# Pre-norm decay attention and mixture of experts on one core: folds on another engine, and another order of the early loads

## What is computed

```
x = x + attn(layernorm(x));  x = x + moe(layernorm(x))

def attn(x):                       # 16 heads of 32
    q, k, v = split(x @ w_qkv, 3)
    q, k = elu(q) + 1, elu(k) + 1
    decay = sigmoid(decay_param)                       # one per head
    run_kv = scan(s = decay * s + k * v over tokens);  run_k = scan(s = decay * s + k)
    den = clip(sum(q * run_k over the head), 1e-6)
    return (q * run_kv / den) @ w_out

def moe(x):                        # 8 experts, the best 2 by softmax, hidden width 352
    scores = softmax(x @ gate_w);  top_w, top_idx = top_k(scores, 2)
    routed = sum over the two of top_w * (silu(x @ w_gate[e]) * (x @ w_up[e])) @ w_down[e]
    shared = (silu(x @ sw_gate) * (x @ sw_up)) @ sw_down      # hidden width 704
    return routed + shared
```

## Time and profile before

| | |
|---|---|
| median of 3 runs | 683.62 us (677.13 to 686.48) |
| the profiled execution | 681.28 us |
| its span in the profile | 679.5 us |
| TensorE busy | 646.2 us (95%) |
| VectorE busy | 416.2 us (61%) |
| ScalarE busy | 267.8 us (39%) |
| GpSimd busy | 222.7 us (33%) |

### The profile page before, as it was taken

How to read it: one execution, slowest core, us unless ns; L and a number is a source line. 1 busy time by engine, 2 the same in 40 slices (tenths; PEclk the granted TensorE clock), 3 DMA queues, 4 the chain that set the end, 5 groups by cost and what they waited for, 6 DMA issues and landing times.

```text
span 679.5 us, 11781 instructions
## 1 busy us (share of the span) xinstructions
PE 646.2 (95%) x3787; PEld 426.7 (63%) x3788; DVE 416.2 (61%) x754; ACT 267.8 (39%) x407; POOL 222.7 (33%) x266
## 2 busy tenths in 40 slices
PE   7989999999999999999998999999999999999991
PEld 7766777767677656666655656666666666666550
DVE  7786987997998755767778776533333333333330
ACT  5363462464453445465665765311111111111110
POOL 6320131231103227222332241244444444434421
PEclk9998999999999999999999999999999999999997
DMA  6840012513425697586684424388777877889852
GB/s 233 309 133 16 15 48 66 167 47 94 125 63 175 185 248 191 160 187 170 162 188 137 72 42 87 65 148 137 133 127 134 137 131 137 133 134 126 136 76 40
DMA packets 110388, 86.89 MB, mean 128 GB/s; under 512 B 79280, under 2 KB 85424, under 8 KB 110352
## 3 DMA queue, kind: packets, MB, share of 16 engines
q1 hardware_dynamic: 88848, 43.94, 27.9%
q0 software_dynamic: 12864, 29.50, 25.5%
q10 hardware_dynamic: 8640, 12.98, 5.8%
HBM read 44.45 MB, written 23.33 MB: 100 GB/s over the span
## 4 chain that ended last, share of the span: by engine, by line
PE 55%; DMA 10%; DVE 7%; issue 3%; ACT 1%; POOL 1%; SPq 1%; POOLq 0%; DVEq 0%; ACTq 0%
PE ps_y L535 15%; PE ps_u L535 14%; PE ps_g L535 14%; PE ring L393 8%; DMA out_dram<-y_job,job_tok 5%; PE turn_h L555 3%; DMA x_in<-x_job 2%; DMA x_job<-xn_scratch,job_tok 2%; DVE routed L1484 1%; DMA xn_scratch<-xn_hl 1%; DMA out_dram<-x 1%; DVE hid L1427 1%; DVE col_max L1463 1%; DVE den L1359 0%; PE ps_norm L410 0%
## 5 line engine op out<-in xcount | busy, mean ns | idle before, releaser
L1145 ACT CAST hidT<-turn_h 128x384 f16<-128x384 f32 x71 | 33.9, 478 | 173.1 <-PE turn_h L555 168.2
L989 POOL DMA_INDIRECT out_dram<-y_job,job_tok x39 | 61.8, 1585 | 98.9 <-DVE y_job L1769 60.0
L393 PE MATMUL ring<-xnT_h,wq_h 128*128 128x512 f32 x192 | 79.4, 413 | 4.2 <-DVE xnT_l L1298 2.0
L535 PE MATMUL ps_y<-routed,hidT 128*128 x351 | 82.1, 379 | 1.3 <-DVE hidT L1420 1.3
L535 PE MATMUL ps_g<-routed,x_in 128*128 x468 | 82.6, 313 | 0.5 <-DMA x_in<-x_job 0.5
L393 PE MATMUL ring<-xnT_h,wq_l 128*128 128x512 f32 x192 | 77.3, 403 | 0.0
L393 PE MATMUL ring<-xnT_l,wq_h 128*128 128x512 f32 x192 | 77.1, 402 | 0.0
L535 PE MATMUL ps_u<-routed,x_in 128*128 x468 | 76.2, 312 | 0.0
L1427 DVE SCALAR_TENSOR_TENSOR hid<-ps_u,job_hid,silu 128x352 f32<-128x352 f32 x39 | 22.8, 584 | 85.5 <-PE ps_u L535 83.3
L535 PE MATMUL ps_y<-shared,hidT 128*128 128x512 f16 x288 | 67.4, 379 | 3.7 <-DVE hidT L1420 3.7
L896 POOL TENSOR_SCALAR var_eps<-mean_var 128x1 f32<-128x1 f32 x32 | 12.3, 384 | 171.9 <-DVE mean_var L1406 93.4
(11 more groups left out here) (246 smaller groups left out, 1095.5 us busy)
## 6 DMA issues: line engine op xcount, KB each, us to landing
x_res<-in_L_attn_x_dram SPq DMA_DIRECT2D x18, 256.0 KB, 3.6
routed<-in_L_ffn_w_gate_dram ACTq DMA_DIRECT2D x6, 704.0 KB, 4.7
routed<-in_L_ffn_w_up_dram ACTq DMA_DIRECT2D x6, 704.0 KB, 6.5
out_dram<-x SPq DMA_DIRECT2D x16, 256.0 KB, 3.5
xn_scratch<-xn_hl SPq DMA_DIRECT2D x16, 256.0 KB, 2.6
out_dram<-y_job POOLq DMA_DIRECT2D x16, 256.0 KB
x_in<-in_L_attn_x_dram SPq DMA_DIRECT2D x14, 256.0 KB, 2.7
routed<-in_L_ffn_w_down_dram ACTq DMA_DIRECT2D x6, 512.0 KB, 7.2
```

The lines of the kernel that those rows point to most:

```text
L393: ins = pe.matmul(ps, a, b, start=(i == 0), stop=(i == len(steps) - 1))
L535: ins = pe.matmul(ps, a[i][:, k, :], w(j, k), start=(start and q == 0), stop=(stop and q == len(steps) - 1))
L989: pool.indirect_dma_start(out[:, :], bass.IndirectOffsetOnAxis(job_tok[:, r:r + 1], 0), y_job[:, b, :], None, compute_op=ALU.add).then_inc ...
L1145: act.copy(hidT[:, 0], turn_h[:, 0:FC, :]).then_inc(s["hidTh_s"], 1)
```

## The change

1. The 16 folds of routed gate and up matrices leave GpSimd; DVE does them at the end of the unit, behind the splits and ahead of the routing work.
2. Part 11 of the projection matrix gets a place of its own (`last_raw`, later used by the last shared down piece), so its load waits for nothing. Parts 12 to 15 wait for low parts by new counts, and the shared down matrix also waits for part 11's low part.
3. x tiles 4 to 7 are loaded ahead of the shared matrices, tiles 6 and 7 into `x_res`; the residual's first two tiles are loaded later, behind x tiles 8 and 9.
4. The four loads of the decay parameters go from GpSimd to ScalarE, as the first thing that it issues.
5. DVE makes the low parts of weight parts 2 and 3 behind those of all four x tiles.
6. The first projection (K of chunk 0) needs the four high parts to start, does its eight products with high weights first, and waits for one low part ahead of each of the last four. The waits of V and Q are as before.
7. In each block DVE makes the low part of the next block's second x tile ahead of `lo_gate` and `max_step`, not behind.

The diff, cut to its core:

```diff
+            if m == QKV_PARTS - 1:
+                return last_raw[:, 0:D]
+            return w_raw[:, (turn_of(m) % 3) * D:(turn_of(m) % 3 + 1) * D]
...
-            return (x_res if t in (2, 3) else x_in)[:, t % 2, :]
+            return (x_res if t in (2, 3, 6, 7) else x_in)[:, t % 2, :]
...
-                if n == 0 and c == 0:
-                    pe.wait_ge(s["w_lo"], KC * {1: 1, 2: 2, 0: 3}[z] - EARLY_W)
-                    pe.wait_ge(s["w_lo_e"], EARLY_W)
+                first = n == 0 and c == 0 and z == 1
+                if first:
+                    pe.wait_ge(s["w_hi"], KC)
+                elif n == 0 and c == 0:
+                    pe.wait_ge(s["w_lo"], KC * {2: 2, 0: 3}[z] - EARLY_W)
...
+                for k, ((wh, wl), (xh, xl)) in enumerate(pairs):
+                    pe.matmul(ps[:, :], wh, xh, start=(k == 0), stop=False)
+                    pe.matmul(ps[:, :], wh, xl, start=False, stop=False)
+                for k, ((wh, wl), (xh, xl)) in enumerate(pairs):
+                    if k < EARLY_W:
+                        pe.wait_ge(s["w_lo_e"], k + 1)
+                    else:
+                        pe.wait_ge(s["w_lo"], k + 1 - EARLY_W)
+                    ins = pe.matmul(ps[:, :], wl, xh, start=False, stop=(k == KC - 1))
...
             def load_x(t):
                 if t >= TPB:
-                    sp.wait_ge(s["xn1"], t - 1)
+
+                    sp.wait_ge(s["xn1"], t - 3 if t < 2 * TPB + 2 else t - 1)
...
             def load_part(m):
-                if m >= FREE_PARTS + 3:
-                    sp.wait_ge(s["w_lo"], m - 2 - EARLY_W)
+                if m >= QKV_PARTS:
+
+                    sp.wait_ge(s["w_lo"], m - 3 - EARLY_W if turn_of(m) < 6 else m - 2 - EARLY_W)
...
-            load_res(0)
-            load_res(1)
-            load_x(TPB)
-            load_x(TPB + 1)
+            for t in range(TPB, 2 * TPB):
+                load_x(t)
...
             sp.wait_ge(s["over_0"], 1)
+            sp.wait_ge(s["w_lo"], QKV_PARTS - EARLY_W)
...
+                if n == 0:
+                    load_x(2 * TPB)
+                    load_x(2 * TPB + 1)
+                    load_res(0)
+                    load_res(1)
...
-            for g in range(P // DH):
-                pool.dma_start(dec[g * DH:(g + 1) * DH, :], bass.AP(decay.tensor, g, [[0, DH], [P // DH, KC]]),
-                               allow_slow_non_contiguous=True).then_inc(s["dec_in"], 16)
...
-                for u in (2 * t, 2 * t + 1):
-                    if norm_unit(u) is not None and pieces[norm_unit(u)][1] < 2:
-                        fold(norm_unit(u))
...
+            for g in range(P // DH):
+                act.dma_start(dec[g * DH:(g + 1) * DH, :], bass.AP(decay.tensor, g, [[0, DH], [P // DH, KC]]),
+                              allow_slow_non_contiguous=True).then_inc(s["dec_in"], 16)
...
             lo_x(1)
-            lo_w(EARLY_W)
             lo_x(2)
-            lo_w(EARLY_W + 1)
             lo_x(3)
-            for m in range(TPB, QKV_PARTS):
+            for m in range(EARLY_W, QKV_PARTS):
                 lo_w(m)
...
                 query(n, 2)
+                next_x(lo_x, 1)
                 if n == 0:
                     lo_gate()
                 max_step(n * KC + 2)
-                next_x(lo_x, 1)
...
-                if norm_unit(u) is not None and pieces[norm_unit(u)][1] == 2:
+                if norm_unit(u) is not None:
                     fold(norm_unit(u))
```

42 lines of the change are left out of this document (22 added, 20 removed).

## The result

The changed kernel took 673.13 us (median of 5 runs, 671.50 to 676.39), the kernel before 684.84 (median of 5 runs, 677.13 to 686.48). The ratio is 0.988, with a 95% interval of 0.984 to 0.992. Beside the first experiments the same two kernels ran again, and gave 672.99 us (6 runs), 681.29 us (14 runs) and a ratio of 0.989 [0.986, 0.993]. The medians of the first pair differ by 11.7 us, more than its ratio says, and those of the second by 8.3. The profiled execution took 676.39 us (span 674.3) against 681.28 (span 679.5) before.

The account below looks back on a forecast made before the run. TensorE was taken as the bound, so time is won only where it stands or runs slowly. 3.4 - 0.3 + 4.2 + 2.7 = 10.0 us off the median of 683.62 gave 673.6 us, range 667 to 681.

Parts of the forecast that it names:

- Start: Up to the first query projection: it starts at 20.1 instead of 23.46 us, 3.4 us won; bounds 0.6 and 3.7.
- x tiles that land clearly later than before: At the kernel's beginning: one of the listed signs that would show the forecast wrong; no size given.
- The decay loads: Moved to ScalarE's queue, they run while the x tiles land: 0.3 us lost, bounds 0 and 2.8.
- The upper bound of 2.8: Loads of decay parameters: 2.8 us per engine if each of 512 four-byte elements cost an average packet of the other queue.
- rival (d): Beginning of the kernel: the decay loads hold up the x tiles, 2.8 in place of 0.3 us, total 676.1; chance 5%.
- Block 0: First block: wait for tile 5's low part shrinks by 2.5 us, clock returns 1.7: 4.2 us won, bounds 1.3 and 4.7.
- Folds: Mixture: folds on DVE save 1.8 us of hidT waits and 0.9 of a fold wait: 2.7 us; upper bound 4.7.
- (a): Mixture: DVE stands at each fold for the square, 16 x 1.59 = 25.4 us lost, total 701.7; chance 3%.
- (b): Value projection: waits 1.3 us or more and runs at 1.2 GHz, 2.8 us lost, total 676.4; chance 14%.
- (c): First block stays bound by DVE and the clock still falls: 1.3 instead of 4.2 us, total 676.5; chance 12%.
- (e): Whole kernel: all waits go, 3.7 + 4.7 + 4.7 = 13.1 us won, total 670.5; chance 10%.
- a threshold between 1.69 and 1.97 us: TensorE's clock: a pause of 1.69 us did not bring it down, only 1.97 and 3.04 did.

Follow-up runs that it names:

- the first experiments: First group of follow-up runs, on one chip with the kernel before: the changed kernel repeated unchanged (ratio 0.989), and e1, e2 and e4, which move the decay loads.
- e5: Changed kernel with the sixteen folds of routed gate and up back on GpSimd; ratio to the kernel before 0.993.
- e2: Changed kernel with the four decay loads issued by SyncE, behind the last part of the projection weights; 672.62 us, ratio to the kernel before 0.987.
- e11: e2 run once more, unchanged, on another chip; median 675.68 us, ratio to the kernel before 0.990.
- e4: Kernel before with only the four decay loads moved, from GpSimd to the head of ScalarE's queue; 684.43 us against 681.29, ratio 1.006.
- e1: Changed kernel with the four decay loads back on GpSimd, behind its low parts of the weights; 672.89 us, ratio to the kernel before 0.988.
- e12: Changed kernel with decay loads behind SyncE's weight parts and each scatter ahead of the gather for the job four later; 692.59 us, ratio to the kernel before 1.017.
- e6: Changed kernel with the low part of the next block's second x tile back behind the gate's low part and column maximum; ratio to the kernel before 0.991.
- e8: Changed kernel with weight part 11 back in the ring of three buffers, its load waiting for part 8's low part; ratio to the kernel before 0.989.
- e9: Changed kernel with x tiles 6 and 7 loaded behind the shared matrices, in the buffers the change gave them; ratio to the kernel before 0.994.
- e10: Changed kernel with decay loads behind SyncE's weight parts and GpSimd making three low parts of the projection weights instead of two; ratio to the kernel before 0.990.

## Why the prediction was right, and where it was not

The time was forecast at 673.6 us and is 673.13. That they agree so closely is partly luck: the ratio makes it 1.2% and 1.1%, about 8.3 and 7.3 us of the time before, where the forecast had 10.0. The marks say the same, with 7.5 and 6.8 us at mark B in the two traces. The forecast was set against a median of 683.62 us for the kernel before, which came out at 684.84 in this measurement and at 681.29 in the next.

**Start: 3.4 us forecast.** The query projection, which follows the value projection's 2.8 us without a wait, starts near 22.6 instead of 23.46: 0.85 us won, and 0.5 in the second trace. The working itself was sound, since without the decay loads it came out at 13.30 and 17.64 against the forecast 13.2 and 17.3. The prediction had named x tiles that land clearly later than before as a sign of being wrong, and they did. The parts that it was built from are each worth something by themselves: undoing the order costs 1.45 us, undoing the buffer 1.80.

**The decay loads: 0.3 us forecast. This is the step that failed.** I put them near the row that showed these very loads, 128 packets on GpSimd's queue. On ScalarE's queue they are 576 packets, and it is not the engine time they take (3.5% from 2 to 10 us) that costs, but what they do to the queue beside them: 1.22 MB in place of 2.38. By the kernel before, the move costs 2.5 us at mark A. With the change made, mark A has a mean of 71.3 over the three traces with this start (71.47, 71.81 and e5's 70.58), and of 69.8 over the three with the loads at SyncE and nothing else changed in the start (69.34, 70.74, 69.29): 1.5 us.

Part of that is the clock during the warm-up, which has to be taken out. In both traces of the changed kernel 14 warm-up matmuls took 1.70 us (1.2 GHz), against 0.94 in e5 and e2. But e11, with the loads away, has the 1.70 too, and is 1.4 us later at mark A than e2, which is the same kernel. Compared at equal clock, mark A is 1.3 us later at the full clock (70.58 against 69.34 and 69.29) and 0.7 to 1.1 at the lower one (71.47 and 71.81 against 70.74). The first projection is 1.5 us later at the full clock (e5's 14.77 against 13.30 and 13.22), of which 1.0 to 1.1 is the late x tile. A warm-up with matmuls at 1.2 GHz behind the first transposes' pause is found in five of the eight traces with the loads at ScalarE's head, where TensorE pauses 1.71 to 2.62 us ahead of its first transposes, and in one of the six others, with pauses of 0.68 to 0.81. So the longer pause may make it more frequent; that is not shown. The marks also miss something: an execution is 2.01 to 2.16 us longer than its span wherever the loads are at ScalarE's head, and 1.71 to 1.84 elsewhere, 0.3 us more that lie outside the span.

The upper bound of 2.8 and rival (d) held the truth, and (d) had got 5%. The Trainium skill (DMA: Bandwidth & Descriptors, Rules for kernel authors) was weighed against the row of GpSimd's queue in the prediction, and the measurement sides with the skill: 576 is 512 four-byte elements and four times 16. The row was of another queue, and that should have made it weigh less.

**Block 0: 4.2 us forecast, 3.9 found** (4.7 at mark A less 0.85, and 4.4 less 0.5). The wait is 0.75 us where 0.55 was forecast, and the clock stays at 1.00 as forecast. Its rows add up: the wait is 2.29 us shorter (3.04 to 0.75, where 2.5 was forecast), and from the transposes behind it to the next ones it takes 3.26 us in place of 4.82, so 1.56 come from the clock (1.7 forecast). What the prediction said of the parts is half right. The order is worth the 1.6 us that was read from DVE's rows. The early x tiles were counted at 1.32 us and are worth 3.7: 2.1 of wait, since DVE gets to the tile earlier than before and would stand for it all the longer, and 1.55 of clock.

**Folds: 2.7 us forecast, 3.5 to 3.9 found** by the single undo. Each step is in the trace: y_scale at 0.16 us, DVE's busy time down though it does more, the wait for a fold 1.69 to 0.34. Both terms were too small: the waits for hidT were forecast to lose 1.8 of 3.0 us and lost 2.6, the wait for a fold 0.9 and lost 1.35. That the whole change shortens the way from A to B by only 2.8 us (325.15 to 322.34), near the 2.7 forecast, is luck: with its folds undone it takes 326.23 there, 1.1 us longer than the kernel before did in its trace. The second trace of that attention and mixture, e4, has 325.79, so part of the 1.1 is the spread between executions, and the rest was not followed up.

**The rivals.** (a), that the folds cost more on DVE: excluded by e5. (b), that the value projection's pause takes the clock with it: that pause was 0.82 to 1.43 us in the eleven traces that have it, and behind it every matmul of the value projection took 0.39 to 0.50 us, as at full clock. (c), that block 0 stays bound by DVE: the wait is 0.75. (d) happened. (e), that all waits go: they did not.

**What the prediction did not see** is what varies behind mark B. Less the waits for gathered tiles, the jobs take 262.5 to 263.4 us in all traces but those of e1 and e12, and on top come these waits, from 0 to 4.5 us, another number in each execution. The changed kernel has 1.56 and 0.67 us of them, the kernel before 0.47. A second part stands behind the last down product, where the last scatters each wait for the one before: from there to the end of the span it takes 13.0 to 16.1 us (e1 left out). The two traces of the changed kernel, which is the same program, reach the last down product at 658.19 and 657.89, and their spans are 674.3 and 670.9: 3.1 of the 3.4 us arise there. Timeline of the last scatter, first trace and second:

```profile
664.91 1.55 POOL L1022 DMA_INDIRECT out_dram<-y_job,job_tok  x1 [3.58 <-DMA out_dram<-y_job,job_tok]
```

```profile
661.70 1.55 POOL L1022 DMA_INDIRECT out_dram<-y_job,job_tok  x1 [3.59 <-DMA out_dram<-y_job,job_tok]
```

Together they can hide 1.5 us won at the start from the whole time. Why the waits for gathered tiles come stays open. The three traces with the decay loads at SyncE and the jobs in their old order have 2.8, 4.1 and 4.5 us, and the others, but for e1 and e12, 2.3 or less. An earlier arrival does not explain it, since e11 arrived no earlier than the changed kernel, and no step was shown that would link the waits to the loads. It would take several traces of each kernel.

## What to carry to other kernels

A load's cost is not its bytes and not the engine time it takes. Four loads of 0.5 KB halved what the queue beside them moved for 8 us, because they stood at the very moment when the first tiles are on their way. Look at what shares the time, and read a row of one queue as evidence for that queue only.

Undoing the parts one at a time gives 1.45, 1.8, 1.6 and 3.7 us up to mark A, 8.5 in all, where the whole change won 4.7 and lost about 1.5 by the decay loads, 6.2 without them. Parts of one chain can be worth more when undone than together: with tile 6 loaded late, its wait also took back what the start had won. Give each the number of the undo, and do not add them.

A mark late in each stage tells apart what the whole time, in which later waits vary by 4 us, does not. Read the way between two marks rather than the time of one: two traces of one kernel differed by 1.4 us at mark A (e2 and e11), but by 0.1 from the first projection to it, and by up to 0.8 from A to B.

## What the runs showed of the hardware

TensorE's clock does not follow from the length of a pause alone. From the first projection on it fell behind pauses of 1.95, 1.97, 2.73, 2.87, 3.04 and 3.53 us, and stayed at 2.4 GHz behind 1.69 and 2.38 us. Ahead of the first transposes it fell at once behind 0.76 (e11), 1.80, 2.50 and 2.62 us, only some matmuls later behind 1.95 and 2.18 (e6, e8), and not at all behind 1.71, 1.75 and 1.82 (e9, e5, e4). (The column of the granted clock is coarse: for 0 to 13.15 us of the changed kernel it says 1.00, though the 14 warm-up matmuls in that stage took 1.70 us in place of 0.94, so near a change the durations of equal rows are the better reading.) The clearest case is one kernel at one place: behind a pause of 0.76 us the 14 warm-up matmuls took 0.94 us in e2 and 1.70 in e11, which is the same code. The prediction had read a threshold between 1.69 and 1.97 us from its rows, and e6 refutes it with 2.38. These traces agree with the Trainium skill (TensorE: Matmul & The Clock Gate, Part 1), which says that the point of change depends on the phase of a free-running monitor and varies from run to run.

A large operation on GpSimd slows what DVE does beside it. DVE's low part of the weights takes 0.62 us alone and 0.90 beside GpSimd's three in e10. The same shows in the folds: a DVE operation on one column took 1.23 us beside GpSimd's fold and 0.16 without it, so that DVE, which took sixteen folds over, was busy for less time from 240 to 412 us (118.70 us, and 121.54 in e5 with the folds back on GpSimd).

The issue of a DMA can take longer when small packets of another queue are in flight. SyncE's four issues of weight parts took 3.74 to 3.91 us in the eight traces with the decay loads at ScalarE's head and 1.85 or 1.86 in the six others, though the instructions are the same.
